# Two state-space layers with two expert layers between them on one core: biases split early, shared experts' second product in fp32, routed results stored by slot and gathered by token

## The chip, the cores and the metric

One NeuronCore of a Trainium2 chip runs the whole program. Its engines are TensorE (PE; its weight loads are PEld), VectorE (DVE), ScalarE (ACT), GpSimd (POOL) and SyncE (SP), which here only issues transfers. They run their own instruction lists and meet at semaphores; direct transfers are issued by SyncE, indirect ones (gather or scatter by a list of indices) by POOL, and all run on the core's 16 DMA engines. TensorE's clock has two granted levels, 2.4 GHz (1.00 in the profile) and 1.2 GHz (0.50). The metric is the device time of the execution in microseconds, lower is better.

## The reference

1024 tokens of width 256 pass four layers, each with a layer norm ahead and a residual add behind (cut):

```python
x = x + attn_a(layernorm(x))   # 32 heads, recurrent state 64 x 128 per head, causal convolutions
x = x + ffn(layernorm(x))      # experts
x = x + attn_b(layernorm(x))   # 64 heads, recurrent state 8 x 128 per head
x = x + ffn(layernorm(x))      # the same experts again

def experts_all(x, g, gb, w1, b1, w2, b2):          # [e,d,f], [e,f], ... f = 128, d = 256
    y = gelu(x @ g + gb, exact) * (x @ w1 + b1)
    return y @ w2 + b2
def ffn(x):
    aff = sigmoid(x @ wa)                            # 16 routed experts
    topk_p, topk_i = top_k(aff, 2);  topk_p = topk_p / sum(topk_p)
    routed = sum over the two chosen experts of topk_p * experts_all(x, r...)
    shared = sum of the two shared experts of experts_all(x, s...)
    return x + shared + routed
```

## The kernel before

The chunks are of 128 tokens, eight in all. The program has four parts in a row: attention a, experts (stage 0), attention b, experts (stage 1).

**Attention a** works through 16 pairs of heads. Each pair needs projections (`product`, L784, three passes of a split fp32r form that stand in for fp32), convolution taps on VectorE, decays, and products within and across chunks. The decays come from rows of cumulated sums: TensorE sums them (L823, L832) and turns them (L827), VectorE copies them out (L1890), SyncE stores them to DRAM (`scratch_a`) and loads each row back, broadcast over 128 partitions (`load_row`). POOL (L2487, L2473) and ScalarE (L1432) make decays from a row. POOL scales the inputs (L2504), which the first state products (L863) need. SyncE's list ahead of that store holds the first weights and, last, the bias tables: `gb` and `ub` as they are, then the same two turned into rows of `scratch_r` element by element (L594), then `b2`.

**An expert stage** starts with norm, transposes and the router's scores (`head`). TensorE computes the two shared experts for both halves of the tokens: four steps, each `up` (L784), then ScalarE's gelu, VectorE's product with the other half (`hidden`, L2057), and `down` (L1015). For `down`, ScalarE and POOL split the hidden values and the weights into high and low parts, and three products are added (`PRODUCTS`). Meanwhile VectorE turns the scores into two choices per token (`route_first`, `route_second`), TensorE ranks the tokens per expert (`rank`, L1026), VectorE gives each choice a slot (`places`), TensorE lists the tokens by slot (`members`, L1037), and VectorE writes the token index of each slot (`tokens`) and, from the same list, where its result goes (`results`). The 2048 choices fill 31 blocks of 128 slots, each of one expert. For each block POOL gathers 128 normed rows from `scratch_v` (L2695), TensorE turns them in (L1066), makes the up product (L1076, L1079), turns the hidden values (L1088) and makes the down product (L1096, L1098), ScalarE does gelu (L1594) and copies the result out (`block_out`, L1601), VectorE the three copies and products between, and POOL scatters the rows to their token's place in `scratch_y` (L2702). A ring of four buffers holds gathered rows, another the results. After the last scatter SyncE loads the results back in token order, VectorE adds them with their shares (`add_experts`, L2263), in stage 0 with the next layer's norm statistics between, in stage 1 with the output behind them. `deviation` on POOL makes the norm factors of two chunks at a time. SyncE also issues in stage 0 the next layer's weights and, after the results, its constants.

All lists are written out by hand in the order in which they run, so what stands behind a waiting instruction of its engine waits too. `keep_busy` issues products of ones with no other use on TensorE; `BUSY_NORM` gives their number ahead of each norm's transposes.

## Time and profile before

| what | value |
|---|---|
| median of 3 runs | 1099.77 us (1099.74, 1099.77, 1107.16) |
| the profiled execution | 1107.84 us, span 1106.5 us |
| granted clock, mean | 0.918 |
| PE busy | 943.3 us (85% of the span) |
| VectorE, ScalarE, POOL busy | 711.6, 583.3, 663.2 us (64%, 53%, 60%) |
| busy tenths of PE, first 200 us in slices of 27.7 us | 7, 8, 1, 0, 3, 9, 9 |
| the chain that ended last | PE 59%, DVE 19%, POOL 6%, SyncE's queue 5%, DMA 4%, issue 4%, ACT 3% |

Start times are from the start of the span. A row of the timeline gives start, length, engine, line, operation, output<-input, shape and count; in brackets stands the idle time just before it and who ended it. A merged row (x3) is several instructions in a row. The parts lie at: start of attention a 0 to 127 us, its pairs until about 640, experts stage 0 until about 797, attention b until about 960, experts stage 1 to the end.

### The profile page before, as it was taken

To read this page: it belongs to the slowest core of one execution; us is meant where nothing else is said; L and a number is where in the kernel's file an instruction comes from. 1 tells how busy PE (TensorE), PEld (TensorE's weight loads), DVE (VectorE), ACT (ScalarE), POOL (GpSimd) and SP (SyncE) were. 2 spreads that over 40 slices of the span, in tenths; PEclk is the share of its full clock that TensorE was granted. 3 is DMA by queue.
4 is the path that set the end of the run, shared out by engine and by line. 5 is a ranking of instruction groups with operands and counts; after the bars stand their busy time and mean duration, and the time that the engine had idled before them with its cause. 6 is when DMAs were issued, how large, how long until landed. Compare 5 with 4: busy or idle time off the path is not lost.

```text
span 1106.5 us, 22666 instructions
## 1 busy us (share of the span) xinstructions
PE 943.3 (85%) x9110; PEld 736.3 (67%) x9110; DVE 711.6 (64%) x1247; ACT 583.3 (53%) x920; POOL 663.2 (60%) x670
## 2 busy tenths in 40 slices
PE   7810399999999999999999996999588886988993
PEld 6600387888888888888888875666466355865661
DVE  5700488888878889787888665432595966354433
ACT  5800488776868777687776350122387444140221
POOL 4600756887867788686786845576238723224772
PEclk9965699999999999999999996799699989995996
DMA  3661321211112212121110571232512115041233
GB/s 109 30 1 5 117 66 68 68 49 68 62 46 66 77 39 77 50 69 57 39 49 2 165 209 36 69 84 47 180 39 63 22 32 150 24 133 53 84 87 116
DMA packets 67092, 77.64 MB, mean 70 GB/s; under 512 B 17139, under 2 KB 55123, under 8 KB 66983
## 3 DMA queue, kind: packets, MB, share of 16 engines
q1 hardware_dynamic: 61037, 63.85, 22.0%
q0 software_dynamic: 5952, 12.34, 4.1%
q8 instruction: 74, 1.21, 0.4%
q14 instruction: 29, 0.24, 0.1%
HBM read 63.65 MB, written 12.55 MB: 69 GB/s over the span
## 4 chain that ended last, share of the span: by engine, by line
PE 59%; DVE 19%; POOL 6%; SPq 5%; DMA 4%; issue 4%; ACT 3%; DVEq 0%; POOLq 0%; ACTq 0%
PE psum L784 20%; PE psum L1079 7%; DVE arena L1907 6%; PE psum L756 4%; PE psum L863 4%; PE psum L1098 4%; SPq L565 4%; PE psum L855 3%; PE psum L908 3%; DVE arena L1944 2%; DMA scratch_a<-arena 2%; SPq L594 1%; PE psum L1066 1%; PE psum L1209 1%; PE psum L1076 1%
## 5 line engine op out<-in xcount | busy, mean ns | idle before, releaser
L784 PE MATMUL psum<-vT,split 128*128 128x512 f32 x1368 | 348.1, 404 | 6.2 <-DVE arena L1907 5.0
L1907 DVE SCALAR_TENSOR_TENSOR arena<-psum,arena 128x1023 f32<-128x1023 f32 (+2 forms) x208 | 265.9, 1278 | 81.1 <-ACT arena L1402 57.5
L784 PEld LDWEIGHTS psum<-vT,split 128*128 128x128 f32 x1368 | 250.0, 189 | 65.6 <-DVE arena L1907 7.1
L1402 ACT ACTIVATE arena<-psum,arena 128x512 f32<-128x512 f32 x160 | 109.2, 690 | 73.9 <-PE psum L784 73.0
L863 PE MATMUL psum<-arena 128*64 128x64 f32 x1792 | 62.5, 225 | 69.1 <-POOL arena L2504 69.1
L863 PEld LDWEIGHTS psum<-arena 128*64 128x64 f32 x1792 | 57.6, 140 | 74.7 <-issue 74.6
L2469 POOL TENSOR_TENSOR split<-arena,split 128x256 fp32r<-128x256 f32 x114 | 83.6, 741 | 33.3 <-ACT split L1327 33.3
L1419 ACT ACTIVATE arena<-arena 128x1024 f32<-128x1024 f32 x80 | 84.4, 1058 | 33.8 <-POOL arena L2496 22.8
L2496 POOL TENSOR_TENSOR arena<-arena,v 128x1021 f32<-128x1021 f32 x32 | 76.3, 2386 | 42.7 <-DVE arena L1907 42.7
L2487 POOL TENSOR_TENSOR bcast<-bcast,arena 128x1024 f32<-128x1024 f32 x32 | 60.8, 1900 | 68.0 <-DMA bcast<-scratch_a 68.0
L2695 POOL DMA_INDIRECT bcast<-scratch_v,arena x62 | 60.6, 978 | 38.4 <-PE psum L1066 13.2
L2209 DVE COPY arena<-psum 128x128 f32<-128x128 f32 x62 | 18.1, 292 | 99.9 <-PE psum L1088 99.9
L1932 DVE TENSOR_TENSOR bcast<-psum,bcast 128x512 f32<-128x512 f32 x64 | 42.4, 683 | 61.8 <-ACT bcast L1432 61.3
L2702 POOL DMA_INDIRECT scratch_y<-bcast,arena x62 | 62.6, 1010 | 32.3 <-ACT bcast L1601 16.8
L756 PE MATMUL psum<-ident,arena 128*128 128x128 f32 x568 | 73.0, 274 | 8.4 <-POOL arena L2526 4.9
L1079 PE MATMUL psum<-arena 128*128 x248 | 79.5, 448 | 0.0
L756 PEld LDWEIGHTS psum<-ident,arena 128*128 128x128 f32 x568 | 64.1, 141 | 20.0 <-POOL arena L2526 8.6
L1432 ACT ACTIVATE bcast<-bcast 128x1024 f32<-128x1024 f32 x32 | 32.2, 1052 | 65.0 <-POOL bcast L2473 64.8
L1594 ACT ACTIVATE arena<-psum 128x128 f32<-128x128 f32 x62 | 17.2, 277 | 87.1 <-PE psum L1079 87.1
L855 PEld LDWEIGHTS psum<-arena 128*128 128x128 f32 x512 | 61.2, 192 | 2.0
L855 PE MATMUL psum<-arena 128*128 128x128 f32 x512 | 62.5, 275 | 0.0
L1079 PEld LDWEIGHTS psum<-arena 128*128 128x128 f32 x248 | 47.0, 211 | 13.0 <-issue 2.4
(275 smaller groups left out, 1804.3 us busy)
## 6 DMA issues: line engine op xcount, KB each, us to landing
bcast<-scratch_a SPq DMA_DIRECT2D x32, 512.0 KB, 3.6
arena<-in_w_a SPq DMA_DIRECT2D x16, 768.0 KB, 4.2
arena<-scratch_y SPq DMA_DIRECT2D x16, 256.0 KB, 4.3
arena<-in_wout_a SPq DMA_DIRECT2D x8, 256.0 KB, 2.6
scratch_v<-v SPq DMA_DIRECT2D x8, 256.0 KB
arena<-in_wg SPq DMA_DIRECT2D x4, 512.0 KB, 5.5
arena<-in_wu SPq DMA_DIRECT2D x4, 512.0 KB, 6.4
arena<-in_wd SPq DMA_DIRECT2D x2, 1024.0 KB, 9.1
```

Of the source, the lines that this page charges most:

```text
L756: m = pe.transpose(bank[:, i * P:(i + 1) * P], src, ident[:, :])
L784: m = pe.matmul(bank, split[:, t % SPLITS, i, q, :], vT[:, j, q, half * BANK:(half + 1) * BANK], start=(n == 0), stop=(n == 3 * KD - 1))
L855: m = pe.matmul(chunk(bank, i), chunk(cv_a[:, j % 2, 1 + g, :], c), chunk(cv_a[:, j % 2, 3 + g, :], c), start=True, stop=True)
L863: m = pe.matmul(out[half, :], lhs[:, half], rhs, start=True, stop=True)
L1079: m = pe.matmul(up_bank, hT_b[:, j % 2, i, :], arena[:, bass.ds(w + i * 2 * F, 2 * F)], start=False, stop=(i == KD - 1), skip_group_check= ...
L1402: act.activation(tile[:, hs], wide_of(t)[:, hs], ACT.Identity, scale=w[:, TAPS - 1:TAPS], bias=0.0).then_inc(sem["tap0"], 1)
L1419: act.activation(tile, tile, ACT.Silu).then_inc(sem["silu"], 1)
L1907: dve.scalar_tensor_tensor(out=tile[:, s:T], in0=bank[:, 0:T - s], scalar=cw_a[:, j, i, TAPS - 1 - s:TAPS - s], in1=tile[:, s:T], op0=ALU. ...
L2469: pool.tensor_tensor(split[:, t % SPLITS, 1], raw, split[:, t % SPLITS, 0].bitcast(F32), ALU.subtract).then_inc(sem["split"], 1)
L2487: pool.tensor_tensor(r3, r3, spread(fac("cumhi", h), P), ALU.subtract).then_inc(sem["expo"], 1)
L2496: pool.tensor_tensor(tile, tile, term_of(j, i)[:, far:T], ALU.add).then_inc(sem["light"], 1)
L2702: pool.indirect_dma_start(scratch_y, bass.IndirectOffsetOnAxis(result[:, j:j + 1], 0), given[:, j % RING, :], None, bounds_check=CHOICES * ...
```

## The change

- **Biases.** The tables `gb` and `ub` are turned by two transposes on TensorE, copied to SBUF by ScalarE, and split into three bf16 parts by ScalarE and POOL during the first two pairs; SyncE stores the parts to `scratch_p` ahead of the rows of the fourth pair. The element-wise stores, `scratch_r` and the way of `b2` through it are gone. `b2` is loaded to SBUF directly.
- **Shared experts.** `down` takes the hidden values and the weights as they are, in fp32: four products a step instead of twelve. The casts and subtractions that made the parts are gone, with their semaphores.
- **Router.** The best expert is the smallest of 1 + exp(-score), without the reciprocal; shares take reciprocals of two values later. VectorE does the second choice before the second hidden product. `rank` stands on TensorE behind the first `down`; ten dummies stand ahead of `members`. The list of members lies in another PSUM bank, and `down` of the second half waits until it has been read.
- **Results.** Each block's results are stored by SyncE as a plain 128-row copy in slot order. POOL issues no scatter; its gathers of a stage stand in a row. After the stores POOL gathers, for each chunk and choice, the 128 rows by slot (`collect`, 16 gathers a stage). In stage 0 two pairs of chunks are collected in the stage, the other two between the norm factors of the next layer.
- **Dummies.** `BUSY_NORM[2][0]` goes from 16 to 45. The next layer's weights are issued later in stage 0, behind the shared biases; POOL makes all of its constants (`fixed`) ahead of the gathers.

```diff
-BUSY_NORM = ((12, 4, 4, 0), (5, 5, 5, 0), (16, 5, 5, 0), (5, 5, 5, 0))
+BUSY_NORM = ((12, 4, 4, 0), (5, 5, 5, 0), (45, 5, 5, 0), (5, 5, 5, 0))
+BUSY_LIST = 10
...
-                for at, name in ((0, "gb"), (F, "ub")):
-                    sp.dma_start(scratch_r[:, at:at + F], io[name].rearrange("f e -> e f"),
-                                 allow_slow_non_contiguous=True).then_inc(sem["braw"], 16)
-                load("braw", scratch_r[:, 2 * F:BIASES], io["b2"])
+                load("b2", raw_bias[:, 2 * F:BIASES], io["b2"])
...
                 for j in range(PAIRS):
+                    if j == 2:
+                        on.wait_ge(sem["bias_p"], 4)
+                        load("bias_s", scratch_p.rearrange("i e n -> e i n"), parts_e)
+                        on.wait_ge(sem["bias_s"], 16)
...
-                for r in range(RING):
-                    on.wait_ge(sem[f"sct{r}"], 16 * n_given(n, BLOCKS - 1, r))
-                for q in range(NC // 2):
-                    for k in range(CHOICES):
-                        at = 1 + k * T + 2 * q * P
-                        load(f"yl{q}", y_e[:, k, 2 * q:2 * q + 2, :],
-                             scratch_y[at:at + 2 * P, :].rearrange("(c p) d -> p c d", c=2))
+                if n == 0:
+                    for part in range(TILES_B + 2):
+                        load_second_layer(part)
+                for j in range(BLOCKS):
+                    on.wait_ge(sem["blk_y"], BLOCKS * n + j + 1)
+                    load(f"sct{j % RING}", scratch_y[j * P:(j + 1) * P, :], given[:, j % RING, :])
...
                     if half == 1:
-                        on.wait_ge(sem["router"], n_router(n, "place"))
+                        on.wait_ge(sem["router"], n_router(n, "result"))
                     for c in range(4 * half, 4 * half + 4):
-                        for m_, (iw, ih) in enumerate(PRODUCTS):
-                            m = pe.matmul(out_cols(c), split_hid[:, s % 2, ih, (c % 4) * P:(c % 4 + 1) * P],
-                                          split_down[:, p % DOWNS, iw], start=(p == 0 and c % 2 == 0 and m_ == 0),
-                                          stop=False, skip_group_check=True)
+                        m = pe.matmul(out_cols(c), hid_e[:, s % 2, (c % 4) * P:(c % 4 + 1) * P],
+                                      w_e[:, p, 2 * KD * F:WORDS], start=(p == 0 and c % 2 == 0), stop=False,
+                                      skip_group_check=True)
...
                 down(0)
+                rank()
                 up(3)
                 down(1)
-                rank()
+                keep_busy(out_cols(6), BUSY_LIST)
+                members()
                 down(2)
-                members()
                 down(3)
+                turn_in(0)
                 shared_bias()
-                turn_in(0)
                 turn_in(1)
...
                 hidden(0)
                 route_first()
+                route_second()
                 hidden(1)
-                route_second()
+                places()
                 hidden(2)
-                places()
+                tokens()
+                results()
                 hidden(3)
-                last_lo()
-                tokens()
                 owners()
-                results()
...
+            def collect(q):
+                for c in (2 * q, 2 * q + 1):
+                    for i in range(CHOICES):
+                        at = i * NC + c
+                        pool.indirect_dma_start(y_e[:, i, c, :], None, scratch_y,
+                                                bass.IndirectOffsetOnAxis(result[:, at:at + 1], 0)).then_inc(
+                                                    sem[f"yl{q}"], 16)
...
-                for j in range(BLOCKS + 2):
-                    if j + RING + 2 < BLOCKS:
-                        gather(j + RING + 2)
-                    if j >= 2:
-                        scatter(j - 2)
+                for r in range(RING):
+                    on.wait_ge(sem[f"sct{r}"], 16 * n_given(n, BLOCKS - 1, r))
+                for q in range(NC // 2 if n else 2):
+                    collect(q)
...
-                deviation(2, 0)
+                for q in range(NC // 2):
+                    deviation(2, q)
+                    if q + 2 < NC // 2:
+                        collect(q + 2)
```

The order of the instructions at three places, as the built programs have it (a row is line, operation, output<-input, shape and count of one or several equal instructions; lines of the change are numbered by its own file). First SyncE's queue at the start, before: the last input loads, the stores of the bias tables, the decay store and the first rows.

```order
L565 DMA wa_e<-in_wa_e 128x32
L565 DMA gb<-in_gb 128x18
L565 DMA ub<-in_ub 128x18
L594 DMA scratch_r<-in_gb 18x128x1
L594 DMA scratch_r<-in_ub 18x128x1
L565 DMA scratch_r<-in_b 18x256
L565 DMA scratch_a<-arena 128x2x128
L565 DMA bcast<-scratch_a 128x1024 x4
```

The same place in the change:

```order
L567 DMA wa_e<-in_wa_e 128x32
L567 DMA gb<-in_gb 128x18
L567 DMA ub<-in_ub 128x18
L567 DMA arena<-in_b 18x256
L567 DMA scratch_a<-arena 128x2x128
L567 DMA bcast<-scratch_a 128x1024 x4
```

One small load stands where three stores to `scratch_r` stood, ahead of the decay store. Second, TensorE in the front of an expert stage, before (L1015 is `down`, L1026 and L1028 `rank`, L1037 `members`, L1044 `shared_bias`), from the second step's `down`:

```order
L1015 MATMUL psum<-split_down,split_hid 128x256 x12
L1026 MATMUL psum<-arena,ones 128x144 x8
L1028 MATMUL psum<-arena,tri 128x128
L1015 MATMUL psum<-split_down,split_hid 128x256 x12
L1037 MATMUL psum<-arena,bcast 128x32 x16
L1015 MATMUL psum<-split_down,split_hid 128x256 x12
L1044 MATMUL psum<-bcast,ones 128x256 x8
```

In the change, from the first step's `down` (L1011; L779 is the last `up`, L758 the dummies):

```order
L1011 MATMUL psum<-arena 128x256 x4
L1022 MATMUL psum<-arena,ones 128x144 x8
L1024 MATMUL psum<-arena,tri 128x128
L779 MATMUL psum<-vT,split 128x512 x12
L1011 MATMUL psum<-arena 128x256 x4
L758 MATMUL psum<-ones 128x128 x10
L1033 MATMUL psum<-arena,bcast 128x32 x16
L1011 MATMUL psum<-arena 128x256 x8
L1062 MATMUL psum<-ident,bcast 128x128 x2
L1040 MATMUL psum<-bcast,ones 128x256 x8
```

The ranks stand an `up` and a `down` earlier, and both products of the second half stand behind the lists. Third, POOL from the gathers of stage 0 to the next layer's norm factors, in the change (L2664 gathers tokens, L2440 collects results, L2424 to L2430 are one pair's norm factors):

```order
L2664 DMA bcast<-scratch_v,arena 128x256 x31
L2440 DMA arena<-scratch_y,arena 128x256 x8
L2424 TENSOR_SCALAR eps_rstd<-bn 128x2
L2425 TENSOR_SCALAR nbias<-bn 128x2
L2428 TENSOR_TENSOR rstd<-eps_rstd,neghalf 128x2
L2430 TENSOR_TENSOR nbias<-nbias,rstd 128x2
L2440 DMA arena<-scratch_y,arena 128x256 x4
```

Before, gathers and scatters (`scratch_y<-bcast,arena`) alternated one by one there, and norm factors followed the last scatter with no transfer between; now 31 gathers, then collects, and the third and fourth pair's collects stand behind the first and second pair's norm factors.

## Rows read from the trace of the kernel before

**Rows 1.** Chain of waits in time order: start us, length us, what; before the pairs.

```profile
39.99 15.20 SPq L594
55.23 34.61 SPq L565
89.88 19.87 DMA scratch_a<-arena
109.77 5.78 DMA bcast<-scratch_a
```

**Rows 2.** Timeline, 30 to 130 us: start, length, engine, line, operation; VectorE, ScalarE, TensorE.

```profile
40.79 1.08 DVE L1890 COPY arena<-psum 128x256 f32<-128x256 f32 x3
...
55.27 1.11 ACT L1410 ACTIVATE v<-psum,arena 128x1021 f32<-128x1021 f32 x1
...
55.33 3.04 PE L784 MATMUL psum<-vT,split 128*128 128x512 f32 x12
127.44 2.83 PE L863 MATMUL psum<-arena 128*64 128x64 f32 x48 [69.08 <-POOL arena L2504]
```

**Rows 3.** Timeline of TensorE, first expert stage, from the shared products to the blocks.

```profile
660.58 1.60 PE L1015 MATMUL psum<-split_down,split_hid 128*128 128x256 f32 x12
...
666.26 0.67 PE L1026 MATMUL psum<-arena,ones 128*128 128x144 bf16 x8
...
677.37 2.93 PE L1015 MATMUL psum<-split_down,split_hid 128*128 128x256 f32 x12 [1.72 <-DVE split_hid L2064]
...
684.61 0.39 PE L1076 MATMUL psum<-arena,ones 3*128 x1 [0.54 <-issue]
```

**Rows 4.** Timeline of VectorE, first expert stage: the router.

```profile
656.11 0.95 DVE L2094 RECIPROCAL arena<-arena 128x128 f32<-128x128 f32 x1
...
662.42 1.57 DVE L2104 TENSOR_TENSOR arena<-arena 128x128 bf16<-128x128 f32 x1
...
675.15 0.74 DVE L2057 SCALAR_TENSOR_TENSOR arena<-psum,ub,arena 128x512 f32<-128x512 f32 x1
...
677.45 0.19 DVE L2155 SCALAR_TENSOR_TENSOR arena<-psum,arena 128x32 int32<-128x32 f32 x1
```

**Rows 5.** Windows, L1079 alone: stretch, us, PE busy, PEld busy, granted clock, DMA.

```profile
684.50:706.50 22.00, 12.21 (x24) 7.05 (x24) 0.50 0.20 57
1006.00:1020.50 14.50, 8.30 (x16) 4.70 (x16) 0.50 0.21 60
1020.50:1080.00 59.50, 27.14 (x96) 16.26 (x96) 1.00 0.30 82
```

**Rows 6.** Timeline of POOL, second expert stage: a gather, its line, its gap.

```profile
1001.65 0.95 POOL L2695 DMA_INDIRECT bcast<-scratch_v,arena  x1 [0.30 <-issue]
```

**Rows 7.** Chain of waits, last 107 us: a gather and a scatter until landed.

```profile
1001.65 3.52 DMA bcast<-scratch_v,arena
...
1091.43 2.11 DMA scratch_y<-bcast,arena
```

**Rows 8.** Timeline, end of the first expert stage: ScalarE, VectorE, POOL.

```profile
771.70 0.37 ACT L1601 COPY bcast<-psum 128x256 f32<-128x256 f32 x1 [1.19 <-PE psum L1098]
...
778.47 1.67 DVE L2263 SCALAR_TENSOR_TENSOR x<-arena,x 128x256 f32<-128x256 f32 x4 [9.38 <-DMA arena<-scratch_y]
...
781.32 0.24 POOL L2455 TENSOR_SCALAR eps_rstd<-bn 128x2 f32<-128x2 f32 x1 [7.49 <-DVE bn L1769]
...
795.56 0.22 POOL L2455 TENSOR_SCALAR eps_rstd<-bn 128x2 f32<-128x2 f32 x1 [4.05 <-DVE bn L1769]
...
796.96 0.20 POOL L2461 TENSOR_TENSOR nbias<-nbias,rstd 128x2 f32<-128x2 f32 x1
```

**Rows 9.** Timeline, all engines, the kernel's end.

```profile
1090.29 0.37 ACT L1601 COPY bcast<-psum 128x256 f32<-128x256 f32 x1 [1.56 <-PE psum L1098]
...
1099.49 4.84 DVE L2263 SCALAR_TENSOR_TENSOR x<-arena,x 128x256 f32<-128x256 f32 x12 [0.74 <-DMA arena<-scratch_y]
```

**Rows 10.** DMA issues, 770 to 800 us: count, KB each, median us to landing.

```profile
split_gate<-arena SPq DMA_DIRECT2D x1, 1024.0 KB, 9.4
```

154 lines of the change are left out of this document (50 added, 104 removed).

## The prediction

> **What bounds the kernel now.** I read the chain of waits in order of time first, then the timelines of single engines where it leaves TensorE, then windows for the granted clock. TensorE carries most of the chain, so what counts is where it stands still, where its clock is at the lower of its two levels (0.50 of 2.4 GHz), and what the end waits for.
>
> The largest hole lies ahead of the sixteen pairs. TensorE ends its work at 58.4 us and starts again at 127.44: 69.08 us idle [rows 2]. The chain shows why: SyncE's queue is held 15.20 us by the second element-wise store of a bias table (L594) and 34.61 us by the small `b2` store behind it; then the decay rows' own store needs 19.87 us to land, and the first broadcast row 5.78 [rows 1]. The data of that store was ready long before: VectorE's three copies end at 41.87 [rows 2].
>
> The second place is the front of each expert stage, where the router's small VectorE steps decide when tokens can be gathered; the first block starts at 684.61 [rows 3, 4]. The granted clock is 0.50 for the first 22.0 us of blocks in one stage and 14.5 us in the other, 1.00 afterwards [rows 5]. Each block has four records on L1079: 6 and 4 blocks at half clock, then 24 in 59.5 us, 2.48 each. In that last stretch TensorE has no gap, while POOL needs a gather and a scatter for each block, about 2 x 1.25 us [rows 6]: close behind, but TensorE sets the pace. **Taking scatters from POOL therefore buys nothing inside the loop.**
>
> The third place is the end of each expert stage. The last block is copied out at 772.07, its results are back and being added from 778.47, and the last pair's norm factors are ready at 797.16 [rows 8]. At the kernel's end the last copy is done at 1090.66, the adds at 1104.33 [rows 9].
>
> **The change, part by part** (against the profiled execution, 1107.84 us with a span of 1106.5; the median of the three runs, 1099.77, is 8 lower, the third run, 1107.16, is not).
>
> *A, the start.* The two element-wise stores and the trip of `b2` through DRAM go; what remains is an 18-row load. The decay store can be issued at 41.9 instead of 89.88. It then lands in 2 to 3 us (2.11 is the nearest row, a 128 KB scatter [rows 7]) and the row needs its 5.78 [rows 1]: there at 50 to 51 instead of 115.55, 65 earlier. What else could be late is near: ScalarE's own work ends at 56.4, TensorE's at 58.4 [rows 2], and ScalarE now does a bias copy and a first bias part ahead of the decays, some 1 to 1.5 us. TensorE would restart at about 63 to 64, not at 62. I take **-63.5**; at most the whole hole, -69, at least -60, if those small steps and POOL's two extra subtractions of 1.2 us each add up. The new bias store on SyncE's queue stands before the rows of the fourth pair, whose buffer comes free later anyway: nothing.
>
> *B, the fronts.* On VectorE a reciprocal goes from the choice of experts (0.95 and its gap), and the second choice follows the first with no hidden product (0.74, as the one at 675.15) between. The mask, ready at 663.99 [rows 4], comes 1.7 earlier. TensorE ranks directly behind the first shared down product, not behind two and an up product: that product is 12 passes in 1.60 us [rows 3]; in fp32 it is 8 passes at 0.28 (27.14 us for 96 [rows 5]), 2.3 us. So ranks start at 660.6 + 2.3 = 662.9, not 666.26: -3.4. Between the lists and the tokens one product of 0.74 stands where two steps took 2.1 (675.15 to the compare ahead of 677.45 [rows 4]): tokens at 672.9, not 677.6. A gather issued 0.9 later lands after 3.52 [rows 7], 677.3; two fp32 down products end at 677.7. Bias and turn-ins follow, about 2.7 at full clock, so blocks start at 680.4, not 684.6: **-4.2 a stage, -8.4**. Bounds: -1 each, if the clock falls, and -5.5. The removed casts and subtractions on ScalarE and POOL were needed only for the three-product form and save nothing by themselves.
>
> *C, the clock.* In the fronts of before the clock fell after TensorE had waited on the router, and the loops began at half clock. In the change, products fill the place of the router's steps (up, down, then ten dummies), and the longest emptiness left is that around the lists, about 3.5 us with 0.7 of work in it. If the clock holds, 6 blocks cost 14.6 instead of 22.0 and 4 cost 9.8 instead of 14.5: **-12.1**; if it falls and stays, 0. I take it as held, since the empty stretch is one and is followed by two dense fp32 products.
>
> Here a rule of the Trainium skill can be weighed. In the trace TensorE works without a break in much of the stretch 684.5 to 706.5, at 0.50 throughout [rows 5]. "TensorE: Matmul & The Clock Gate", section "What's actually happening", says that a busy array is given the full clock back. This trace does not agree for the block loop; by that rule a fall would cost a stage only a few us and the forecast would be nearly safe, by the row it costs 5 to 7.
>
> *D, the end of the first expert stage.* The copy-out ends at T (772.07). SyncE's store lands at T+2.1, as the scatter's. Then POOL collects: 4 gathers a pair of chunks, 1.25 apart [rows 6], each landed 3.52 after its start [rows 7]. The first pair is there at T+9.4 (before: T+6.4). POOL is free at T+12.1, its norm steps for pair one start at T+12.2, since 2.85 pass between first add and norm (778.47 to 781.32), and take 1.6 (795.56 to 797.16 [rows 8]). Alternating so, the third pair is landed at T+21.1, the fourth at T+27.7, and the last norm ends at T+32.1 instead of T+25.1: +7.0. SyncE issues the next layer's constants (two loads of 1 MB, one of them [rows 10], and three smaller) right behind its last store, at the same time as the collects; that costs more, unknown from before. Low: nothing. High: landings as slow as the 9.4 us of such a constant [rows 10], +8. I take +2, nearer the low end, as only the first two pairs meet them: **+9**. The 45 dummies end before the first transposes can start and hide behind this wait.
>
> *E, the kernel's end.* All 16 collects stand in a row: store 2.1, fifteen steps of 1.25, a landing of 3.52 and four adds of 1.67 make 26.0 us from the last copy to the last add; before it is 1104.33 - 1090.66 = 13.7. **+12.3**, between +10 (a store landed sooner, the adds overlapping the landings) and +16.
>
> Sum: -63.5 - 8.4 - 12.1 + 9 + 12.3 = -62.7, so **1045 us**. The two ends give back more than POOL, ScalarE and the fp32 products save; the gain is the start's.
>
> **Rivals.**
> 1. *The clock falls in the fronts all the same.* For it: the router's waits were enough for it in both stages, and once low it stayed for six and four blocks. Against: fewer and shorter waits. One stage loses about 10 (its part of C and most of B): 1054; both: 1065. Chance 0.28, of which both 0.08.
> 2. *The constants hold up the collects.* "DMA: Bandwidth & Descriptors", section "Queues, rings and completion order", says that each DMA engine takes turns between its queues; no row of before shows collects beside constants. As a mechanism here: with the queues sharing, the first two pairs land 3 to 6 us later, POOL stands at the first norm with the other collects queued behind it, and all later pairs move by that. By rows 10 in place of 3.52: D becomes +13 to +15, 1050. Chance 0.07.
> 3. *The start is repaired by halves.* If the decay store is slow by itself (19.87 us [rows 1]), only SyncE's 50 us are won: 1060. Against it: 128 KB land in 2.11 elsewhere. Chance 0.04.
> 4. *Slower: collects are served one by one.* If POOL can start a collect only when the one before has landed, a step is 3.52 + 0.3 instead of 1.25: 32 of them cost 82 more. Then 1127. It decides from 3.2 us a step on ((1108 - 1045) / 32 on top of 1.25). Gathers of before, from another tensor, run 1.25 apart, which speaks against it. Chance 0.01.
>
> **Numbers.** Forecast 0.60, its own range 1035 to 1052. With rivals 2 and 3 and the one-stage case of rival 1 the range is 1034 to 1062. A measurement of this kernel can tell about 1%, 11 us, from no change: faster 0.98, within 0.01, slower 0.01.
>
> **What would show it.** A: SyncE's queue free of anything above 1 us before 42 us, and TensorE's idle at the pairs' start under 6 us. B: from the affinities to the first block 25 instead of 29 us. C: granted clock 1.00 when blocks start, 2.44 to 2.48 us from the first steady block on. D and E: POOL rows of 1.25 us in fours with norms between, and 16 in a row at the end, 26 us from last copy to last add. Wrong if the hole at the start shrinks by less than 55, if blocks start at 0.50, or if a collect's step is above 1.5 us.

## The result and the profile after

The changed kernel takes **1033.95 us** (median of four runs, 1031.37 to 1037.16) against 1101.35 for the kernel before on the same chip: ratio 0.938, interval 0.933 to 0.943. The forecast was 1045 with a range of 1034 to 1062, so the time is 11 us under the forecast and 0.05 us outside the range's low end. The mechanisms were the ones forecast; the size of the largest, the start, was not, and with it the fronts' and the loops'. The profiled execution took 1031.37 us with a span of 1030.1, 76.4 less span than the 1106.5 of before.

I cut both spans at the same places, so that each difference is one of the prediction's terms. "First block" is the first product of the block loop (L1072, before L1076), "last copy" the end of ScalarE's last block copy, "layer" TensorE's first product on L779 (before L784) behind the last norm, "norm" the first dummy product (L758, before L763) ahead of an expert stage's norm.

| stretch | before, us | after, us | difference | forecast |
|---|---|---|---|---|
| start to norm, stage 0 | 640.10 | 571.04 | -69.1 | -63.5 (A) |
| norm to first block, stage 0 | 44.51 | 38.23 | -6.3 | -4.2 (B) |
| first block to last copy, stage 0 | 87.46 | 78.58 | -8.9 | -7.4 (C) |
| last copy to the second layer | 26.45 | 37.14 | +10.7 | +9 (D) |
| second layer to norm, stage 1 | 162.59 | 160.21 | -2.4 | 0 |
| norm to first block, stage 1 | 45.11 | 37.92 | -7.2 | -4.2 (B) |
| first block to last copy, stage 1 | 84.44 | 78.49 | -6.0 | -4.7 (C) |
| last copy to the end | 15.84 | 28.49 | +12.7 | +12.3 (E) |

**The start**, timeline of the changed kernel, SyncE's queue and TensorE:

```profile
41.34 0.40 SPq L567 DMA_DIRECT2D scratch_a<-arena  x1
43.20 1.76 SPq L567 DMA_DIRECT2D bcast<-scratch_a  x4
...
55.65 3.07 PE L779 MATMUL psum<-vT,split 128*128 128x512 f32 x12
59.55 1.85 PE L858 MATMUL psum<-arena 128*64 128x64 f32 x56 [0.83 <-ACT arena L1434]
```

The decay store is issued at 41.34 instead of 89.88, the rows' loads 1.86 behind it (19.87 before [rows 1]), and TensorE waits 0.83 us where it waited 69.08 [rows 2]. What ends that last wait is a copy on ScalarE, not a transfer.

**The front of the first expert stage**, timeline, VectorE and then TensorE:

```profile
586.80 0.24 DVE L2065 TENSOR_SCALAR arena<-arena 128x128 f32<-128x128 f32 x1 [2.85 <-ACT arena L1592]
...
591.96 0.70 DVE L2075 TENSOR_TENSOR arena<-arena 128x128 bf16<-128x128 f32 x1
...
602.20 0.19 DVE L2126 SCALAR_TENSOR_TENSOR arena<-psum,arena 128x32 int32<-128x32 f32 x1
...
593.25 0.66 PE L1022 MATMUL psum<-arena,ones 128*128 128x144 bf16 x8
...
598.40 2.39 PE L758 MATMUL psum<-ones 128*128 128x128 f32 x20
...
601.47 0.36 PE L1033 MATMUL psum<-arena,bcast 128*128 128x32 f16 x8 [0.48 <-DVE bcast L2116]
602.75 3.69 PE L1011 MATMUL psum<-arena 128*128 128x256 f32 x16 [0.92 <-DVE arena L2146]
606.83 0.44 PE L1062 MATMUL psum<-ident,bcast 128*128 128x128 f32 x2 [0.39 <-DMA bcast<-scratch_v,arena]
...
609.27 0.28 PE L1072 MATMUL psum<-arena,ones 3*128 x1 [0.67 <-issue]
```

From VectorE's first step on the affinities (586.80) to the first block (609.27) are 22.5 us; before it was 655.85 to 684.61, 28.8. The ranks (L1022) stand directly behind the first shared down product, the ten dummies are L758, and the four waits of TensorE in this front (0.48, 0.92, 0.39, 0.67) sum to 2.5 us.

**The clock in the loop**, windows of L1075 alone (columns as in [rows 5]):

```profile
609.20:615.50 6.30, 3.39 (x12) 2.03 (x12) 1.00 0.40 103
615.50:685.00 69.50, 31.66 (x112) 18.97 (x112) 1.00 0.36 97
```

The clock is 1.00 from the first block. The first three blocks take 2.1 us each, the other 28 take 2.44 to 2.48.

**The end of the first expert stage**, timeline, ScalarE, POOL, VectorE; then the DMA queues from 688 to 702 us (busy tenths of the 16 DMA engines, then count, KB each, median us to landing):

```profile
687.48 0.37 ACT L1587 COPY bcast<-psum 128x256 f32<-128x256 f32 x1 [1.79 <-PE psum L1094]
...
690.46 0.94 POOL L2440 DMA_INDIRECT arena<-scratch_y,arena  x1 [20.45 <-DMA scratch_y<-bcast]
...
703.26 0.37 POOL L2424 TENSOR_SCALAR eps_rstd<-bn 128x2 f32<-128x2 f32 x1 [3.13 <-DVE bn L1747]
...
723.16 0.20 POOL L2430 TENSOR_TENSOR nbias<-nbias,rstd 128x2 f32<-128x2 f32 x1
...
700.41 1.67 DVE L2232 SCALAR_TENSOR_TENSOR x<-arena,x 128x256 f32<-128x256 f32 x4 [16.15 <-DMA arena<-scratch_y,arena]
```

```profile
DMA  0091299999999999999999999999999999993830
...
split_hid<-arena SPq DMA_DIRECT2D x1, 1024.0 KB, 5.9
split_gate<-arena SPq DMA_DIRECT2D x1, 1024.0 KB, 9.0
...
scratch_y<-bcast SPq DMA_DIRECT2D x1, 128.0 KB, 1.7
arena<-scratch_y,arena POOLq DMA_INDIRECT x8, 5.7
```

The first collect starts 2.6 us after the last copy's end (687.85), eight stand 1.25 apart; but the first four have landed only at 700.41, 12.6 after the last copy, because 2.75 MB of the next layer's constants keep the DMA engines at 90% or more for eleven of these 14 us. The last norm ends at 723.36, 35.5 after the copy; before it was 25.1 [rows 8].

**The kernel's end**, timeline, POOL and VectorE:

```profile
1004.17 0.94 POOL L2440 DMA_INDIRECT arena<-scratch_y,arena  x1 [20.31 <-DMA scratch_y<-bcast]
...
1023.09 0.94 POOL L2440 DMA_INDIRECT arena<-scratch_y,arena  x1 [0.30 <-issue]
...
1026.22 1.67 DVE L2232 SCALAR_TENSOR_TENSOR x<-arena,x 128x256 f32<-128x256 f32 x4 [3.13 <-DMA arena<-scratch_y,arena]
```

Sixteen collects 1.25 apart, and the last add ends at 1027.89: 26.3 us after the last copy (1001.61), against 13.7 before [rows 9].

### The profile page after: what moved, and what is told of

The parts are those of the page before. It is cut to its first block, busy times and chain, and to the rows that moved or that the text cites. A ratio compares the mean times of both kernels' runs of the same rounds, so it can differ in the third digit from the quotient of the medians.

```text
span 1030.1 us, 22719 instructions
## 1 busy us (share of the span) xinstructions
PE 937.6 (91%) x9178; PEld 737.2 (72%) x9178; DVE 705.5 (68%) x1243; ACT 577.7 (56%) x909; POOL 620.3 (60%) x630
## 4 chain that ended last, share of the span: by engine, by line
PE 60%; DVE 19%; POOL 8%; ACT 7%; issue 4%; DMA 2%; DVEq 0%; POOLq 0%; ACTq 0%
PE psum L779 21%; PE psum L1075 6%; DVE arena L1886 6%; PE psum L751 5%; PE psum L858 4%; PE psum L1094 4%; PE psum L850 4%; PE psum L903 3%; POOL arena L2440 2%; DVE arena L1923 2%; PE psum L1072 1%; PE psum L1092 1%; PE psum L1062 1%; PE psum L1206 1%; PE psum L1240 1%
## 5 line engine op out<-in xcount | busy, mean ns | idle before, releaser
L779 PE MATMUL psum<-vT,split 128*128 128x512 f32 x1368 | 347.7, 404 | 7.6 <-DVE arena L1886 5.2
L779 PEld LDWEIGHTS psum<-vT,split 128*128 128x128 f32 x1368 | 249.6, 189 | 66.9 <-DVE arena L1886 7.1
L2664 POOL DMA_INDIRECT bcast<-scratch_v,arena x62 | 59.5, 960 | 80.8 <-PE psum L1062 70.5
L1416 ACT ACTIVATE arena<-arena 128x1024 f32<-128x1024 f32 x80 | 84.4, 1058 | 31.3 <-POOL arena L2473 19.9
L1075 PE MATMUL psum<-arena 128*128 x248 | 70.1, 405 | 0.0
L850 PEld LDWEIGHTS psum<-arena 128*128 128x128 f32 x512 | 61.2, 192 | 2.0
L2440 POOL DMA_INDIRECT arena<-scratch_y,arena x32 | 30.8, 964 | 49.6 <-DMA scratch_y<-bcast 40.8
L1587 ACT COPY bcast<-psum 128x256 f32<-128x256 f32 x62 | 23.1, 373 | 56.4 <-PE psum L1094 56.4
L2481 POOL TENSOR_TENSOR arena<-arena 128x512 f32<-128x512 f32 x32 | 34.0, 1063 | 31.4 <-DVE arena L1903 31.3
L1641 ACT ACTIVATE bcast<-psum 128x512 f32<-128x512 f32 x52 | 28.3, 603 | 39.8 <-PE psum L1170 39.7
```

What stands on the lines that cost most here:

```text
L779: m = pe.matmul(bank, split[:, t % SPLITS, i, q, :], vT[:, j, q, half * BANK:(half + 1) * BANK], start=(n == 0), stop=(n == 3 * KD - 1))
L850: m = pe.matmul(chunk(bank, i), chunk(cv_a[:, j % 2, 1 + g, :], c), chunk(cv_a[:, j % 2, 3 + g, :], c), start=True, stop=True)
L1075: m = pe.matmul(up_bank, hT_b[:, j % 2, i, :], arena[:, bass.ds(w + i * 2 * F, 2 * F)], start=False, stop=(i == KD - 1), skip_group_check= ...
L1416: act.activation(tile, tile, ACT.Silu).then_inc(sem["silu"], 1)
L2664: pool.indirect_dma_start(gathered[:, j % RING, :], None, scratch_v, bass.IndirectOffsetOnAxis(token[:, j:j + 1], 0)).then_inc(sem[f"gth{j ...
```

## The experiments

Chips differ here more than kernels do, so each group of runs is told by its kernel before: 1101 us on the chip of the result above, 1105.7, 1100.3 and 1102.4 in groups 2, 3 and 6, but 1129.7, 1136.4 and 1130.3 in groups 1, 4 and 5. The six groups ran on six chips; which chip the result above had is not on record. The first four times belong to what will be called the first kind of chip, the others to the second. Where one group has no run of the changed kernel, a comparison with it crosses chips.

**1. The start alone** (groups 1 and 3; the biases' turn is left out).

```diff
-for at, name in ((0, "gb"), (F, "ub")):
-    sp.dma_start(scratch_r[:, at:at + F], io[name].rearrange("f e -> e f"), ...)
+    load("braw", scratch_r[:, at:at + F], io[name].rearrange("f e -> (f e)").rearrange("(e f) -> e f", f=F))
```

> The kernel before with one edit: the two bias tables are stored to DRAM row by row as they lie, not element by element turned round, with the same bytes (so this kernel leaves out the turn of the biases and adds the wrong ones). My theory: the whole hole ahead of the pairs hung on these stores, so this edit alone gives what the start gave in the changed kernel, 68 to 69 us (TensorE at the pairs at about 60 us instead of 127.4, its idle there under 2 us), and nothing anywhere else: ratio to before 0.937 to 0.940. By the step of my prediction 63.5 us: 0.942. Rival (the decay store is slow by itself, only the queue is won): about 48 us, 0.956.

> The kernel before with both bias tables stored as they lie (the turn of the biases is left out, as in the first run of this edit), beside the others of this group. 68 us less than the kernel before: TensorE at the pairs at 59 to 60 us; 1036 to 1040 on a chip like the first, ratio 0.938.

Measured: 1059.9 against 1129.7, ratio 0.936 [0.930, 0.943]; and 1033.13 against 1100.29, ratio 0.940 [0.936, 0.945]. TensorE reaches the pairs at 59.34 and 59.21, the affinities are stepped on at 586.6 and 586.5 as in the changed kernel (586.8). The start is worth 67 to 70 us, the whole hole. TensorE at the start of the pairs in the second run:

```profile
59.21 1.85 PE L863 MATMUL psum<-arena 128*64 128x64 f32 x56 [1.39 <-POOL arena L2504]
```

On a chip of the first kind this edit alone (1033.1) gives all that the whole change gives (1034.0, 1031.8): **everything else in the change sums to about nothing,** as the forecast had it (+0.8), to within the few us by which chips and executions differ (the ratios are 0.940 against 0.938 and 0.932). Both its block loops begin at a granted 0.50 and take 82 us there. On the second kind they take 95 and 94, and the rest of the change is worth 26 us and more (1059.9 here, 1031.7 to 1033.5 in experiments 4 and 8).

**2. One table of two** (group 3; one table's turn is left out).

```diff
-for at, name in ((0, "gb"), (F, "ub")):  # both turned
+sp.dma_start(scratch_r[:, 0:F], io["gb"].rearrange("f e -> e f"), ...)
+load("braw", scratch_r[:, F:2 * F], <ub as it lies>)
```

> The kernel before with one of the two bias tables stored element by element, as before, and the other as it lies (its biases are the wrong ones). The stores of both tables, the small one behind them and the decay store end 70.8 us after the first is issued (38.96 to 109.75). Theory 1 (the elements are worked off one after the other at that rate, 15.4 ns each, and whatever comes behind on the queue waits for them to be written): with half of them the decay store lands at about 74 us, TensorE starts the pairs at about 92, and the kernel gains half, 34 to 36 us, though SyncE itself may be held hardly at all, as the first table alone took 0.98 us to issue. Theory 2 (only a full queue holds things up, and one table fits): the decay store lands within a few us of its issue, and the whole 68 us are gained.

Measured: 1079.33, ratio 0.982 [0.978, 0.987], 21 us gained. Timeline of SyncE's queue and TensorE:

```profile
39.26 0.98 SPq L593 DMA_DIRECT2D scratch_r<-in_gb  x1
40.29 15.43 SPq L565 DMA_DIRECT2D scratch_r<-in_ub  x1
...
56.50 0.47 SPq L565 DMA_DIRECT2D scratch_a<-arena  x1
85.27 2.18 SPq L565 DMA_DIRECT2D bcast<-scratch_a  x4
...
102.89 3.25 PE L864 MATMUL psum<-arena 128*64 128x64 f32 x56 [44.65 <-POOL arena L2505]
```

Neither theory's number came out. The small store behind the one table is held 15.43 us, as the second table was in [rows 1], and the decay store takes 28.8 us from issue to landing. From the first table's issue to that landing are 46 us; with two tables it was 70.8. So the data behind do wait (theory 1's mechanism), but the time does not go with their number: the first table costs more than its half, and TensorE gains 24.5 us at the pairs, not 36.

**3. The changed kernel again** (groups 2 and 4), and the kernel before for its trace (group 2).

> The changed kernel itself, beside the others of this group: 1034 us (1030 to 1040), both block loops 78.5 us from first product to last copy, whatever the chip, since its loop has one indirect transfer a block.

> The changed kernel itself, beside the others of this group: 1028 to 1037; the spread is the clock at the loops' starts, 4 us for each start at half clock.

> The kernel before itself, for its trace on the chip that the other runs of this group share. In the first group its time was 1129.7 us where the first chip gave 1101, while the changed kernel's variants took the same 1031 to 1033 as there. My theory: up to the first expert stage its landmarks are those of the first chip within 1 us; the block loops (87.5 and 84.4 us there) are what varies with the chip, because POOL's two indirect transfers a block leave the loop no room: 95 us or more each if this chip is like the second. The rival: the difference lies at the start (element-wise stores slower) and the loops are the same.

Measured: the changed kernel 1031.81 (ratio 0.932 [0.925, 0.939]) and 1034.27 (ratio 0.908 [0.904, 0.913]). The kernel before, traced in group 2, took 1107.58; it reached the affinities 5.6 us later than in the first trace (661.44), made that up in its first loop (81.9 instead of 87.5), and its second loop was the same 84.4. Its chip was of the first kind, so the kernel before was never traced on the other. Experiment 1 has the same loops, though, and on both kinds: 82.3 and 82.1 us in group 3, 95.0 and 94.4 in group 1. That is 25 us of the 29 by which the kernel before is slower in group 1 than in group 3. In group 2 the changed kernel's first loop began at half clock (windows, L1075):

```profile
609.30:619.60 10.30, 6.22 (x12) 3.52 (x12) 0.51 0.24 64
```

It took 82.0 us instead of 78.58.

**4. No list dummies** (group 1): `BUSY_LIST = 10` becomes 0.

> The changed kernel with the ten dummy products behind the second shared down product left out, nothing else. If these dummies hold TensorE's clock over the lists (my step C), the clock falls in one or both fronts, blocks start at a granted 0.50 and the kernel loses 5 to 15 us against the changed one (1039 to 1049). The rival: the clock held because the fp32 down products stand around a shorter gap, and the dummies hide nothing: within 2 us of 1034.

Measured: 1033.45 (1030.84 to 1039.47), not told apart from the changed kernel. In the trace the clock is 0.50 at the first loop's start and 1.00 at the second's; experiment 6 shows why one trace says little there. What the dummies do shows in the fronts: the first stage's two down products behind the lists take 5.38 us instead of 3.69, and the clock has fallen inside both fronts, which last 23.4 and 23.9 us instead of 22.5 and 22.3. In this trace the ten dummies are worth 1.0 and 1.6 us a stage, not the 5 to 15 expected.

**5. The ranks later** (group 3).

```diff
 down(0)
-rank()
 up(3)
 down(1)
+rank()
 keep_busy(out_cols(6), BUSY_LIST)
```

> The changed kernel with the ranks behind the second up product and the second shared down product, where the kernel before has them, instead of ahead of both; everything else as changed. My step B gave this order 3.4 of the 4.2 us of each front. The products passed take 3.05 and 1.89 us, so ranks end about 5 us later and VectorE's places, lists and tokens with them, less what TensorE still had to wait for: first block 3.4 to 5 us later after the affinities (26 to 28 instead of 22.5), in each stage, and a longer wait on the lists, in which the clock may fall: 1041 to 1050. If the front hangs on something else (gathers, products), under 1 us a stage.

Measured: 1042.05, ratio 0.947 [0.942, 0.952]. From affinities to first block 28.6 and 28.5 us instead of 22.5 and 22.3: 6.1 a stage. Timeline of TensorE:

```profile
599.62 0.66 PE L1022 MATMUL psum<-arena,ones 128*128 128x144 bf16 x8
...
606.73 0.37 PE L1033 MATMUL psum<-arena,bcast 128*128 128x32 f16 x8 [4.11 <-POOL arena L2658]
...
609.05 5.98 PE L1011 MATMUL psum<-arena 128*128 128x256 f32 x16 [0.88 <-DVE arena L2146]
...
617.13 0.28 PE L1072 MATMUL psum<-arena,ones 3*128 x1 [0.54 <-issue]
```

The ranks start at 599.62, TensorE then waits 4.11 us for the marked lists, and the two down products take 5.98 instead of 3.69: the clock has fallen inside the front. So the order is worth 6.1 and 6.2 us, all that B gained, and 2.3 of them are clock. Both loops of this trace run at 1.00 from the start (78.0 us each): behind the longest wait of any changed front the clock fell early, and was back before the first block.

**6. A spare scatter a block** (groups 2 and 6), and **a spare gather** (group 6). Nobody in the loop waits for either.

```diff
-for j in range(BLOCKS): gather(j)
+for j in range(RING + 2): gather(j)
+for j in range(BLOCKS + 2):
+    if j + RING + 2 < BLOCKS: gather(j + RING + 2)
+    if j >= 2: spare(j - 2)
```

> The changed kernel, with one more indirect transfer a block on POOL in the loop: 128 rows of a tile scattered to DRAM of its own, which nobody reads and nobody in the loop waits for. It has the POOL time and the DMA load of the scatters of before, but not their place between copy-out and buffer reuse. Theory 1 (POOL's pace): gather and scatter take 2.6 us a block against TensorE's 2.44, six gathers ahead, so the loops grow from 78.5 to 80 to 84 us each and the kernel to 1037 to 1045. Theory 2 (the scatters themselves, by their landing, stall who waits for them): here nobody waits, loops 78.5 to 80, 1034 to 1037. Theory 3 (POOL late makes TensorE wait, TensorE's clock then falls inside the loop): loops of 90 and more, 1055 and up.

> The changed kernel with one spare scatter a block that nobody waits for, again. On a chip of the first kind (before: 1100) it took 1037, its loops 83 and 85 us with the clock low at both starts. If this chip is of the second kind (before: 1124 to 1140): theory 1, a ring or a wait on the landing makes the loops slow there: nobody waits here, so loops of 79 to 85 us and 1034 to 1042. Theory 2, the scatters as such hold up the signals between the other engines there: loops of 90 to 100 us and 1055 to 1075.

> The same with a spare gather (from the token rows into a free tile) in place of the spare scatter, so POOL has as much to do and DRAM is only read. If on a chip of the second kind any second indirect transfer a block disturbs, loops of 90 to 100 us as with the scatter; if only scattered writes do, 79 to 85 us. On a chip of the first kind both about 79 to 85.

Measured: 1037.21, then 1033.63 and, with gathers, 1038.82, on chips of the first kind. Windows of TensorE around the first loop's start, the same kernel in group 2 and in group 6:

```profile
609.30:620.00 10.70, 10.13 (x26) 0.50 0.23 61
620.00:640.00 20.00, 20.00 (x86) 0.93 0.47 138
```

```profile
609.30:620.00 10.70, 9.64 (x45) 1.00 0.40 103
620.00:640.00 20.00, 20.00 (x92) 1.00 0.51 160
```

The program is the same to the last instruction, TensorE reached the first block at 609.29 and 609.37 us, and one time the loops ran at 0.50 for their first 11 us and more (83.4 and 85.0 us), the other time at 1.00 throughout (78.0 and 78.0). POOL's second transfer cost the loop nothing. (With gathers the loops took 80.8 and 78.4 us; what else that kernel loses stands behind them: its first collect starts 6.0 and 5.7 us after the last copy instead of 2.6, behind its wait for the last store, and the last add ends at 34.7 and 29.6 us instead of 33 and 26.5.) **The clock at the loop's start is a toss in the changed kernel**: of the twelve traces with its fronts and ten dummies, it was 1.00 at the first loop in six and at the second in ten. With the fronts of before (experiments 1 and 2, and both traces of before) it was 0.50 within the first half microsecond in ten starts of ten.

**7. No norm dummies** (group 3): `(45, 5, 5, 0)` becomes `(0, 5, 5, 0)`.

> The changed kernel without the 45 dummy products ahead of the norm between the layers (the kernel before has 16 there). In the text of the prediction they hide behind the wait for the collected rows. If they do and hold no clock that matters, nothing: 1032 to 1036. If they keep TensorE's clock for the transposes and projections that follow, those start at a granted 0.50 and cost 1 to 5 us more.

Measured: 1044.37, ratio 0.948 [0.943, 0.954]. Windows of TensorE over the first 10 us of the second layer (from its first product on L779), this kernel first, then the changed one:

```profile
731.30:741.30 10.00, 8.96 (x44) 1.00 0.00 0
```

```profile
725.00:735.00 10.00, 8.95 (x45) 1.00 0.01 2
```

The layer begins at a granted 1.00 with the dummies and without, and so it does in every trace of this document. From the last copy to the last add it is 32.6 us without them and 32.7 with, and from the layer's first product on, VectorE's steps start within 0.1 us of each other for 94 us. **In the wait and right behind it the 45 dummies buy nothing.** From the last add of stage 0 to the affinities of stage 1 this kernel does take 185.8 us, against 176.8 to 180.9 in the nine traces of the changed kernel and its variants that collect behind the loop; but it loses the difference in the layer's second half, where TensorE stands idle for nothing that the profile shows. What TensorE waited for in the last 80 to 86 us of that stretch (us, times, longest), this kernel, then the changed one:

```profile
PE psum L1206 <- issue: 5.3, 3, 2.2
PE psum L1240 <- issue: 3.6, 1, 3.6
```

```profile
PE psum L1206 <- issue: 5.3, 2, 3.5
```

Such stops of over half a microsecond sum to 10.8 us in this trace's layer, to 4.1 to 6.9 in the fourteen other traces with 45 dummies, and to 7.0 to 10.7 in the five with 16. Their cause is open; whether the dummies far ahead of them have a part in it, no run tests. The rest of this trace's loss are two loops that began below full clock (85.0 and 83.4 us), and the first of them stands ahead of the dummies. All four executions (1038.75 to 1048.5) are slower than any of the changed kernel's, so the loss of some 10 us is real, but the wait and the clock behind it, as expected, are not its cause.

**8. The constants later** (group 1): SyncE waits for the second pair's rows before the constants.

> The changed kernel with SyncE waiting for the second pair's collected rows before it issues the next layer's constants. If these transfers held up the first collects (rival 2 of the prediction), the first adds come about 6.5 us after the last copy instead of 12.6, and the first norm then stands behind POOL's own queue, so the last norm comes 2.5 to 3.5 us sooner: 1031. If the collects are late for another reason, the same 1034 with the first adds where they are. If the constants are needed sooner than I think, slower by up to 8 us.

Measured: 1031.66 (1030.17 to 1039.68). First adds 10.1 us after the last copy instead of 12.6 to 13.2, last add 31.0 instead of 32.7 to 33.3. In this trace the constants cost about 2 us at that end; the time is not told apart from the changed kernel's.

**9. The scatters kept** (groups 1, 2 and 4): all of the change but its results' path.

```diff
-load(f"sct{j % RING}", scratch_y[j * P:(j + 1) * P, :], given[:, j % RING, :])  # SyncE, each block
-for q in ...: collect(q)                                                         # POOL, after the loop
+scatter(j)                                                                       # POOL, each block
+load(f"yl{q}", y_e[...], scratch_y[...])                                         # SyncE, after the loop
```

> The changed kernel with the results' path of the kernel before: each block scattered per token by POOL inside the loop, contiguous loads by SyncE in the tail, norms one after the other. The two ends should give back what they cost: 10.4 us at the end of the first expert stage and 12.6 at the kernel's end. In the loop POOL then has 2 x 1.25 us a block against TensorE's 2.44, which could cost up to 3 us a stage. My theory: 1011 to 1017 us, ratio to before 0.918 to 0.923. The rival (POOL's scatters become the bound of a loop that now starts at full clock): blocks at 2.6 us or more, 1020 and up.

> The changed kernel with the scatters of before kept in the loop, once more, beside the changed kernel on the same chip. In the first group it took 1037 instead of the 1011 to 1017 that I expected: its ends gave back the 23 us, its loops took 98.6 and 92.2 us instead of 78.5. If that belongs to the second chip, a chip like the first gives 1015 here; if it belongs to the scatters in a loop that starts at full clock, 1030 to 1040 again.

> The changed kernel with the scatters of before, a third time. On chips where POOL's two transfers a block fit into the loop (one of the two seen so far): 1006 to 1012, 24 us less than the changed kernel. On a chip like the other: 1033 to 1042, loops of 92 to 99 us, and not less than the changed kernel.

Measured:

| group | before | changed | scatters kept | its two loops, us |
|---|---|---|---|---|
| 2 | 1105.7 | 1031.81 | **1007.82** (1006.34 to 1012.44) | 78.0, 78.1 |
| 1 | 1129.7 | not run | 1037.44 (1032.76 to 1042.62) | 98.6, 92.2 |
| 4 | 1136.4 | 1034.27 | 1038.60 (1035.03 to 1048.62) | 92.9, 96.6 |

The ends gave back what was expected everywhere: last add 22 us after the last copy instead of 33, and 13.7 to 14.0 at the end instead of 26.3. On a chip of the first kind this version beats both kernels, by 98 and by 24 us. On the other kind its loops lose it again. Windows of TensorE from 640 to 660 us, group 2 and group 4, and what TensorE's first product of a block waited for in the first loop (us, times, longest):

```profile
640.00:660.00 20.00, 20.00 (x93) 1.00 0.29 84
```

```profile
640.00:660.00 20.00, 17.26 (x66) 0.85 0.23 69
```

```profile
PE psum L1077 <- issue: 0.6, 1, 0.6
```

```profile
PE psum L1077 <- issue: 9.2, 11, 1.6
```

On the first kind TensorE is never idle there and the clock is 1.00. On the other it stands 9.2 us for nothing that the profile shows, and the clock falls on and off inside the loop.

**10. Sixteen dummies** (group 4): experiment 9 with `BUSY_LIST = 16`.

> The same with 16 dummy products behind the second shared down product instead of ten. If the ten stand at the edge of what holds the clock (same instruction stream, 1.00 in one look and 0.51 in another), 16 hold it in both stages in every run: a narrower spread, 1006 to 1009, though six more dummies of 0.12 us could make the lists wait 0.7 us a stage. If the clock hangs on something else, the same spread.

Measured: 1042.66 (1039.23 to 1045.73) beside 1038.60 with ten: no gain. Both loops of its trace begin at 1.00, as both do in the trace with ten, and their own stalls (99.9 and 92.4 us long) cover the question.

**11. Eight buffers** (group 5, second kind): experiment 9 with a ring of eight between copy and scatter.

```diff
-given = bcast[1].rearrange("p (r d) -> p r d", r=RING)
+given(j) = (bcast[1], bcast[2])[j // RING % 2], buffer j % RING; eight semaphores
```

> The changed kernel with the scatters kept, and with eight buffers instead of four between the copy-out and the scatter (the second four in a tile that is free during the loop). On the two chips where the loops took 92 to 99 us, ScalarE's copy started about 10.1 us after the scatter from the same buffer, four blocks before, whenever it was late: a scatter seems to need 9 to 10 us to land there, and four blocks of TensorE are 9.76. If that is the cause, eight buffers make the loops 78 to 82 us there too, and the kernel 1006 to 1016 on either kind of chip (the kernel before being 1100 or 1130 to 1136 shows the kind). If the landing is not it (POOL's or the gathers' pace, or the memory), such a chip gives 1030 to 1042 as with four.

Measured: 1033.93 (1028.20 to 1041.91), loops 97.7 and 93.6. The theory is refuted: the copies were late again, and already those of the fifth and sixth block, which wait for no buffer at all. (In both slow traces of experiment 9 the same two copies are the first late ones, by 1.5 to 1.6 us.) Timeline around the fifth, TensorE, ScalarE, VectorE:

```profile
628.63 0.70 PE L1107 MATMUL psum<-arena 128*128 x2
...
629.47 1.13 PE L1088 MATMUL psum<-arena 128*128 x4
630.43 0.27 PE L1097 MATMUL psum<-ident,arena 128*128 128x128 f32 x1
...
633.64 0.28 PE L1085 MATMUL psum<-arena,ones 3*128 x1 [1.45 <-issue]
...
630.76 0.37 ACT L1600 COPY bcast<-psum 128x256 f32<-128x256 f32 x1 [2.29 <-PE psum L1107]
632.91 0.28 ACT L1593 ACTIVATE arena<-psum 128x128 f32<-128x128 f32 x1 [1.77 <-remote]
...
632.94 0.29 DVE L2195 COPY arena<-psum 128x128 f32<-128x128 f32 x1 [2.60 <-remote]
```

The fifth block's product ends at 629.33, and ScalarE, with nothing else to do, copies it at 630.76; elsewhere such a copy follows 0.04 us behind. ScalarE's next step waits for L1088, done at 630.60, VectorE's for L1097, done at 630.70, and both start 2.3 us later, within 0.03 us of each other. What the trace shows is an engine that goes on 1.4 us after what it waits for is done, and then two that go on 2.3 us after, at the same moment; whether the signal came late or the engines took it late, its rows do not tell. Why only in loops with scatters, and only on three of the six groups' chips, stays open; the two runs meant for it (experiment 6, group 6) met a chip of the first kind.

## Why the prediction was right, and where it was wrong

**A, mis-sized by 5.6 us; the step that failed.** The prediction put TensorE's restart "at about 63 to 64, not at 62" and took -63.5. It came at 59.55, -67.9, and by the first expert stage -69.1, at the far bound. From POOL's first use of the row to TensorE's restart it is 11.8 us in both kernels (115.61 before, 47.68 after), so what was read too high lies ahead of it: the store landed in 1.8 us and the row in 3.7, 5.6 together (41.34 to 46.94), not 8 to 9. The 5.78 of [rows 1] stood right behind the element-wise stores, as did the 5.75 of experiment 2; with both tables stored as they lie (experiment 1, group 3) the row takes 3.9. The "small steps" that were to sum up fit beside TensorE's own work but for the last 0.83. The last 1.2 us are the clock: the first 56 products took 1.85 us (59.55), and before, behind 69 us of idleness,

```profile
127.44 3.09 PE L863 MATMUL psum<-arena 128*64 128x64 f32 x56 [69.08 <-POOL arena L2504]
```

(the 2.83 of [rows 2] is the same row cut off after 48 of them). Experiment 1 isolates all of it at 67 to 70.

**B, right in kind, too small.** -6.3 and -5.5 measured from the affinities, -4.2 forecast and -5.5 its bound. The ranks' place was given 3.4; experiment 5 gives it 6.1. I moved VectorE's steps by 3.4 and let everything behind them follow; but the slot steps then run beside the last up and the second down product and the long list step (3.21 us) beside the dummies, so that TensorE's wait on the lists (4.11 us in experiment 5) goes too, and the clock holds. And an fp32 down product takes 1.85, not the 2.3 that I took from the block products of [rows 5].

**C, right in these traces, but a toss.** Forecast -12.1, measured -14.8 in the profiled execution, of which about 0.35 in each of the first three blocks is their own speed (2.1 us). I called the clock held since the empty stretch was short. Experiments 3 and 6 show the same program on both sides, at 2 to 7 us a stage; that both starts were at 1.00 in the profiled execution is luck. The clock's part of rival 1 was therefore no rival but belongs to the ordinary spread of the changed kernel, 1028 to 1038; B's part of it did not occur.

**The second layer, missing from the sum, cause open.** The prediction put everything from the first stage's last norm to the second's at nothing. From the last add to the next affinities are 3.8 us less than before in the profiled execution (184.0 to 180.2): the table's row has 2.4 of them, the second front 1.7 of its 7.2. Experiment 7 shows that the dummies do not bring back the clock for it: with 0, 16 and 45 of them the layer's first 60 us take the same to 0.4 us. The difference arises in the layer's second half, with TensorE's unexplained stops (9.9 us before, 5.3 after), and other traces of the same stretch vary by as much: 180.2 to 184.0 with the fronts of before, 176.8 to 180.9 with the changed ones where results are collected (185.8 in experiment 7).

**D and E, right.** +10.7 against +9, of which the constants take about 2 (experiment 8), as taken, and the collects and norms 8.7 against 7.0; +12.7 against +12.3. Rival 2's mechanism is real (experiment 8 takes it away), but its price of +13 to +15 was 2 to 4 too high, since after the late first pair POOL's own queue sets the rest.

**"Taking scatters from POOL buys nothing inside the loop": right on one kind of chip, wrong on the other.** Experiments 6 and 9 show it right on the first kind. On the second kind the scatters cost 14 to 20 us a loop, together more than the 23 us of the collects at both ends. There the change's ratio is 0.908, not 0.938.

**Rivals 3 and 4** did not occur: a store of 1.86 us, a collect's step of 1.25.

In sum the error is A's 5.6, the fronts' 5.1, the loops' 2.7 and the layer's 2.4, less 2.1 of the two ends: 13.7 against the profiled execution. Medians tell it more simply. The forecast stood on an execution of 1107.84, 6.5 above the median of 1101.35; the medians differ by 67.4 where the forecast had 62.7, and experiment 1 gives 67.2 and 69.8 of that to the start alone. So by the medians the error is A's, and the rest of the profiled pair's, 5.1, 2.7 and 2.4, is in part the spread of clock and stops. The range was also cut closer than its own bounds: A at -69, B at -5.5 a stage, C at -12.1, D at +7 and E at +10 give 1032.7.

## What to carry over

A store whose source is read element by element holds up whatever is queued behind it, far beyond its own issue time: look for the first row behind such a store, and price a repair at the whole hole, bounded by what the engines had to do anyway. A path that moves work out of a loop to its end costs its full length there; whether the loop pays it back may depend on the chip, so compare on more than one before choosing. The granted clock at the start of a dense loop can differ between executions of one program, by 2 to 7 us a loop here, and so can an engine's unexplained stops: before a difference of that size is given to a change in one trace, lay the two traces side by side from a common start and see where they part.

## What the runs showed of the hardware

- **Two kinds of chip.** The kernel before took 1092 to 1113 us in the groups of one kind and 1124 to 1143 in those of the other, the changed kernel 1028 to 1038 on both. What goes with the difference is the scatters in the loop (78 us a loop on one kind, 92 to 100 on the other); what it is in the chip stays open.
- **The clock's return.** From 609.30 to 620.00 TensorE was busy 10.13 of 10.70 us at a granted 0.50 (experiment 6). The forecast weighed the Trainium skill's page "TensorE: Matmul & The Clock Gate", section "What's actually happening", which says that a busy array is given the full clock back; by these rows too it does not get it at once, and [rows 5] had it low for 22 us. After a fall at a loop's start in the changed kernel and its variants it was back 7 to 17 us later.
- **An indirect transfer's issue costs POOL the same** whatever its direction: mostly 0.94 to 1.02 us and a gap of 0.30, in gathers, scatters and collects, on both kinds of chip (single ones take 1.1 and more).
- **Element-wise stores do not add up.** One table of 2304 elements and what was behind it took 46 us, two took 70.8 (experiment 2).
